# Q's and K's copies on ScalarE in the first self-attention, and an earlier context split, Q transfers on two queues and a second PSUM bank for V at the cross-attention's begin

## The reference

```python
x = x + L0_xattn(layernorm(x), ctx)       # x @ W1.T + mean(ctx) @ W2.T + b
x = x + L0_attn(layernorm(x), ...)        # 16 heads of 32, causal band of 128
x = x + L0_ffn(layernorm(x), ...)         # 16 experts, top 4, and a shared one
x = x + L1_xattn(layernorm(x), ctx, ctx)  # softmax over the 256 queries (axis=1)
x = x + L1_attn(layernorm(x), ...)        # windows of 128, shifted by 64
x = x + L1_ffn(layernorm(x), ...)         # 8 experts, top 2

# L0_attn
q, k, v = split(x @ Wqkv.T + bqkv)
probs = softmax(where(band, q @ k.T / sqrt(32), -inf))
y = (probs @ v) @ Wo.T + bo

# L1_xattn
Q = query @ Wq + bq;  K = ctx @ Wk + bk;  V = ctx @ Wv + bv
attn = softmax(einsum('bihd,bjhd->bijh', Q, K) * SCALE, axis=1)
out = einsum('bijh,bjhd->bihd', attn, V) @ Wo + bo
```

## Time and profile before

| | kernel before |
|---|---|
| runs (us) | 2662.23, 2661.63, 2662.91; median 2662.23 |
| profiled execution (us) | 2662.88 |
| its span, first to last instruction (us) | 2661.2 |
| mean granted TensorE clock (1 is full) | 0.992 |
| busy (us): PE, PEld | 2608.1, 2202.5 |
| busy (us): DVE, ACT, POOL | 1971.5, 1862.7, 1272.0 |
| chain of waits that ended last | PE 95%, DVE 2%, ACT 1%, DMA 1% |

### The profile page before, as it was taken

The page is one execution under the profiler, slowest core; times in us unless marked ns, Lnnn a source line. Parts: engine busy times, 40 slices in busy tenths (PEclk is TensorE's granted clock), DMA queues, the critical chain, the costliest instruction groups (busy, mean ns, idle before and its releaser), DMA issues.

```text
span 2661.2 us, 59615 instructions
## 1 busy us (share of the span) xinstructions
PE 2608.1 (98%) x21096; PEld 2202.5 (83%) x21096; DVE 1971.5 (74%) x3890; ACT 1862.7 (70%) x6826; POOL 1272.0 (48%) x2199
## 2 busy tenths in 40 slices
PE   8998999899999999999999999999999998999998
PEld 6875999788888888888888888888888885799997
DVE  8876866577787777787777787777787776655555
ACT  2213444288888888888888888888888886355553
POOL 4532111165655565655665655656655653222222
PEclk9998999999999999999999999999999999999999
DMA  9992554556666656666666666666666652545451
GB/s 385 388 396 97 196 190 167 135 154 182 157 161 173 164 157 160 165 162 167 161 166 158 158 169 168 160 158 168 154 164 168 167 130 109 187 177 190 184 190 72
DMA packets 132301, 473.34 MB, mean 178 GB/s; under 512 B 31128, under 2 KB 31256, under 8 KB 124832
## 3 DMA queue, kind: packets, MB, share of 16 engines
q1 hardware_dynamic: 122400, 451.69, 57.9%
q10 hardware_dynamic: 9600, 17.83, 1.8%
HBM read 244.47 MB, written 17.30 MB: 98 GB/s over the span
## 4 chain that ended last, share of the span: by engine, by line
PE 95%; DVE 2%; ACT 1%; DMA 1%; issue 0%; POOL 0%; ACTq 0%; SPq 0%; DVEq 0%; POOLq 0%
PE PB L587 21%; PE PB L612 15%; PE PB L620 14%; PE PB L600 14%; PE PB L688 7%; PE PB L703 6%; PE PB L416 6%; PE PB L549 6%; PE PB L562 3%; PE PB L445 1%; PE PB L476 1%; DMA AR<-in_ctx 1%; ACT EE L832 1%; PE PB L452 1%; PE PB L497 0%
## 5 line engine op out<-in xcount | busy, mean ns | idle before, releaser
L832 ACT ACTIVATE EE<-PB,small 128x256 f32<-128x256 f32 x3136 | 1445.1, 482 | 204.8 <-DVE small L1217 191.4
L1217 DVE TENSOR_REDUCE small<-PB 128x2 f32<-128x512 f32 x1568 | 1031.5, 682 | 355.3 <-PE PB L612 355.1
L832 ACT ACTIVATION_READ_ACCUMULATOR EE<-PB,small 128x1 f32 x3136 | 665.0, 212 | 0.0
L1478 POOL TENSOR_TENSOR VS<-V,small 128x128 f32<-128x128 f32 x784 | 320.5, 409 | 689.4 <-DVE small L1223 682.1
L587 PE MATMUL PB<-CTX,WKV 128*128 128x256 f32 x4704 | 624.7, 282 | 3.1 <-POOL CTX L1466 3.1
L587 PEld LDWEIGHTS PB<-CTX,WKV 128*128 128x128 f32 x4704 | 588.1, 190 | 3.4 <-POOL CTX L1466 3.3
L612 PEld LDWEIGHTS PB<-QS,STK 128*128 128x128 f32 x3136 | 469.1, 190 | 122.0 <-issue 79.9
L612 PE MATMUL PB<-QS,STK 128*128 128x256 f32 x3136 | 555.1, 288 | 5.3 <-ACT EE L832 5.2
L600 PE MATMUL PB<-WKV,CTX 128*128 128x512 f32 x1584 | 433.9, 396 | 3.0 <-DVE V L1213 3.0
L620 PE MATMUL PB<-EE,VS 128*32 128x256 f32 x6272 | 381.4, 384 | 0.0
L600 PEld LDWEIGHTS PB<-WKV,CTX 128*128 128x128 f32 x1584 | 274.0, 191 | 40.0 <-DVE V L1213 3.9
(11 more groups left out here) (201 smaller groups left out, 2546.3 us busy)
## 6 DMA issues: line engine op xcount, KB each, us to landing
STK<-KHL SPq DMA_DIRECT2D x1568, 128.0 KB, 2.5
RW<-in_l1f SPq DMA_DIRECT2D x32, 2048.0 KB, 8.1
AR<-in_ctx SPq DMA_DIRECT2D x49, 1024.0 KB, 8.5
RAW<-in_ctx SPq DMA_DIRECT2D x98, 512.0 KB, 3.7
WF<-in_l0f SPq DMA_DIRECT2D x17, 2304.0 KB, 8.9
v_scr<-RAW ACTq DMA_DIRECT2D x64, 256.0 KB, 7.6
V<-v_scr SPq DMA_DIRECT2D x64, 256.0 KB, 2.9
WA<-in_l0a SPq DMA_DIRECT2D x1, 4096.0 KB, 13.9
```

What stands on the lines that cost most here:

```text
L832: m = e.activation(EE[:, b, s, :], bank(2 * (k % 2) + half, 256 * (s % 2), 256), ACT.Exp, bias=nm[:, b, s:s + 1], accum_out=su[:, b, s:s + 1])
L1217: e.tensor_reduce(nm[:, k % RING, 2 * half:2 * half + 2], bank(2 * (k % 2) + half).rearrange("p (s i) -> p s i", s=2), axis=AX.X, op=ALU.m ...
L1478: e.tensor_tensor(VS[:, b, :].rearrange("p (s d) -> p s d", s=4), V[:, t % 4, 128 * c:128 * c + 128].rearrange("p (s d) -> p s d", s=4), r ...
```

## The change

It has two parts, in different stages.

*First self-attention.* The eight copies of Q and K move from VectorE to ScalarE for u = 0: five ahead of the first exponentials, two between those of chunk 0 and 1, one between those of chunk 1 and 2. ScalarE applies scale before bias, so the bias of Q is multiplied by SCALE once, on GpSimd (`bq`). VectorE's list is maxima, reciprocals and V's copies alone. TensorE projects the first half of V before the last scores. ScalarE's first FFN split moves behind all exponentials, GpSimd's behind the diagonals.

*Cross-attention's begin.* The high half of context group 2 is made right after Q is split, before the low halves of K (and GpSimd's low half, which waits for it, so can run then). Q's transfers: SP issues strips 0 to 2 (12 transfers), ScalarE strip 3 (4 transfers) between and behind its copies of K. The second V (n = 1) uses bank 7, so its matmuls wait for an old copy of bank 7 (`k_lo` 4) and no longer for the first V's copy. The bias of X is added at k = 8 and 9 of the loop.

```diff
+        bq = sb("bq", [P, NC])
+        VBANK = {1: 7}
-        def stack_q(e, half):
-            for s in range(2 * half, 2 * half + 2):
-                for q in range(4):
+        def stack_q(e, s, quarters):
+            for q in quarters:
 # sync_program
-            stack_q(e, 0)
+            for s in range(3):
+                stack_q(e, s, range(4))
 # tensor_program, attention(A)
                     if c + 1 < NC:
                         project(c + 1, 0)
+                    elif u == 0:
+                        values(0)
                     scores(c)
-                values(0)
+                if u:
+                    values(0)
                 values(1)
 # tensor_program, project_v(n, part)
-                    if n:
+                    if n == 1:
+                        w.wait_ge("k_lo", 4)
+                    elif n:
                         w.wait_ge("v_out", n)
-                    m = e.matmul(bank(5), CTX[:, g % 3, xh, c, j:j + 128], WKV[:, 2 + wh, c, :],
+                    m = e.matmul(bank(VBANK.get(n, 5)), CTX[:, g % 3, xh, c, j:j + 128], WKV[:, 2 + wh, c, :],
 # scalar_program, attention(A)
+                def project_out(c, qk):
+                    w.wait_ge("qk_mm", 8 * u + 2 * c + qk + 1)
+                    src = bank(6 + qk, 0, 256)
+                    if qk:
+                        m = e.activation(A.KT[:, c, :], src, ACT.Identity, bias=BC[:, A.ck + c:A.ck + c + 1])
+                    else:
+                        m = e.activation(A.QT[:, c, :], src, ACT.Identity, bias=bq[:, c:c + 1], scale=SCALE)
+                    m.then_inc(S["qk_out"], 1)
+
+                after = ((2, 1), (3, 0)), ((3, 1),), (), ()
+                if u == 0:
+                    w.wait_ge("d_bc", 16)
+                    w.wait_ge("bq_scaled", 1)
+                    for c, qk in ((0, 0), (0, 1), (1, 0), (1, 1), (2, 0)):
+                        project_out(c, qk)
...
+                    if u == 0:
+                        for p in after[c]:
+                            project_out(*p)
 # scalar_program
             move_xt(1)
+            attention(attn[0])
             split0(0, 0)
-            attention(attn[0])
             split0(0, 1)
...
-                if ch == 1:
+                if ch:
                     w.wait_ge("q_split", 1)
-                    stack_q(e, 1)
+                    stack_q(e, 3, ((0,), (1,), (2, 3))[ch - 1])
 # vector_program, attention(A): the old list stands under "else"
+                if u == 0:
+                    maxima(0)
+                    maxima(1)
+                    reciprocals(0)
+                    maxima(2)
+                    reciprocals(1)
+                    values_out(0)
+                    maxima(3)
 # vector_program, before and in the loop
+            split_hi(2)
             for ch, kb in enumerate(KBANK[1]):
                 k_lo(1, ch, kb)
             for n in range(2):
                 v_out(n)
-            w.wait_ge("d_bi0", 32)
-            for i in range(2):
-                e.tensor_tensor(X[:, i, :], X[:, i, :], BI[:, BSLOT[R_XO], :], ALU.add).then_inc(S["x_xbias"], 1)
-            split_hi(2)
...
+                if k in (8, 9):
+                    w.wait_ge("d_bi0", 32)
+                    e.tensor_tensor(X[:, k - 8, :], X[:, k - 8, :], BI[:, BSLOT[R_XO], :], ALU.add).then_inc(S["x_xbias"], 1)
 # gpsimd_program
+            w.wait_ge("d_bc", 16)
+            e.tensor_scalar(bq[:, :], BC[:, C_L0Q:C_L0Q + NC], SCALE, None, ALU.mult).then_inc(S["bq_scaled"], 1)
...
-            w.wait_ge("ln_xn", 4)
+            attention(attn[0])
             split0(0)
-            attention(attn[0])
             split0(1)
```

More of the change, by code:

```diff
@@ L43 @@
 wkv_hi wv_dve wv_pool wk_pool sums early_hi early_lo early_mm early_out p1_mm x_bias mean_rhs mean_mm x_mean
-qk_mm qk_out av_mm av_out x_abias sc_mm sc_max sc_exp sc_rcp diag turn_mm turn_out amix_mm amix_out ao_mm x_attn
+bq_scaled qk_mm qk_out av_mm av_out x_abias sc_mm sc_max sc_exp sc_rcp diag turn_mm turn_out amix_mm amix_out ao_mm x_attn
 f0_xs f0_xs_act f0_hi f0_lo f0_plo f0_up f0_silu f0_mul f0_hhi f0_hlo f0_dn f0_acc gate_mm gate_sig gate_comb
@@ L245, in build @@
         lg1, rk1, t81 = (small[:, o:o + 16] for o in (112, 128, 144))
-        def stack_q(e, half):
-            for s in range(2 * half, 2 * half + 2):
-                for q in range(4):
-                    e.dma_start(
-                        QS[32 * q:32 * q + 32, s, :, :].bitcast(F32),
-                        QHL[32 * s:32 * s + 32, q // 2, :, :].bitcast(F32)).then_inc(S["d_q"], 16)
+        def stack_q(e, s, quarters):
+            for q in quarters:
+                e.dma_start(
+                    QS[32 * q:32 * q + 32, s, :, :].bitcast(F32),
+                    QHL[32 * s:32 * s + 32, q // 2, :, :].bitcast(F32)).then_inc(S["d_q"], 16)
         def sync_program(e):
@@ L1011, in attention @@
                 w.wait_ge(f"d_bi{BSLOT[A.rv]}", 16 * (u + 1))
-                project_out(0, 0)
-                project_out(0, 1)
-                project_out(1, 0)
-                maxima(0)
-                project_out(1, 1)
-                project_out(2, 0)
-                maxima(1)
-                project_out(2, 1)
-                project_out(3, 0)
-                reciprocals(0)
-                maxima(2)
-                project_out(3, 1)
-                maxima(3)
-                reciprocals(1)
-                values_out(0)
+                if u == 0:
[6 more added lines that the diff above has]
+                    maxima(3)
+                else:
+                    project_out(0, 0)
+                    project_out(0, 1)
+                    project_out(1, 0)
+                    maxima(0)
+                    project_out(1, 1)
+                    project_out(2, 0)
+                    maxima(1)
+                    project_out(2, 1)
+                    project_out(3, 0)
+                    reciprocals(0)
+                    maxima(2)
+                    project_out(3, 1)
+                    maxima(3)
+                    reciprocals(1)
+                    values_out(0)
                 reciprocals(2)
@@ L1212, in v_out @@
                     w.wait_ge("vs", 4 * (t - 4) + 4)
-                e.tensor_tensor(V[:, t % 4, :], bank(5), BI[:, BSLOT[R_XV], :], ALU.add).then_inc(S["v_out"], 1)
+                e.tensor_tensor(V[:, t % 4, :], bank(VBANK.get(n, 5)), BI[:, BSLOT[R_XV], :], ALU.add).then_inc(S["v_out"], 1)
             def maxima(k, half):
```

## The result

| | median us | lowest to highest | runs |
|---|---|---|---|
| before | 2661.63 | 2661.04 to 2662.91 | 9 |
| changed | 2655.65 | 2650.19 to 2656.52 | 9 |

The ratio is 0.9974, with the interval 0.9965 to 0.9983: 6.0 us faster by the medians, 6.9 by the ratio. That is as forecast in sign and within the range (2650.5 to 2656.8), 2.05 us above the forecast. New is the scatter: 6.3 us between runs, where before had 1.9.

A forecast was written before the change was run, and what follows sets the result against it. TensorE was taken as the bound (95% of the chain of waits), with nothing to gain in the long loop. 3.2 us (first self-attention) plus 5.4 (cross-attention's begin) made 8.6 off 2662.23: 2653.6 us, range 2650.5 to 2656.8.

The forecast's parts named there:

- Part A: First self-attention: ScalarE copies Q and K, half of V projected before the last scores; 3.2 us gained, bounds 2.0 and 3.6.
- The 0.4 us wait of the third scores: First self-attention: TensorE ready at 222.2, ScalarE's copy of K chunk 2 done at 222.6, so 0.4 us of waiting stays.
- The 0.2 us for VectorE's lateness: End of first self-attention: VectorE's last maxima, reciprocal and V copy make the turned blocks 0.2 us late, leaving 3.2 of 3.4.
- The waits of 2.22 and 3.08: Cross-attention's begin: TensorE's waits for V's bank (2.22 us) and context group 2's low half (3.08 us) would both go.
- part B: Cross-attention's begin: reordered copies, split and Q transfers start mixing at 523.7 instead of 529.18; 5.4 us gained.
- Q's landing: Cross-attention's begin: TensorE waits for all 16 Q transfers, set by bandwidth; first scores at 515.9, bounds 513.4 and 518.
- rival 1: Cross-attention's begin: issue sets Q's end, Q lands early at 514.1, no clock lost; gain 11.5 us, 2650.7; chance 0.12.
- the clock: Cross-attention's begin: after 2.5 us idle TensorE runs at 1.2 GHz once; 1.0 us lost, bounds 0 and 1.7.
- The bracket before the first scores: Cross-attention: sign to look for, a TensorE wait of 2 to 2.5 us with a DMA as its releaser.
- 2 (Q at 518): Cross-attention's begin: SP's last pieces land late, first scores at 518, full slow stretch behind; gain 5.9 us, 2656.3; chance 0.15.
- 3: First self-attention: K's copy waits behind exponentials instead of maxima, half the gain (1.6); with Q late too, 2657.9; chance 0.08.
- 4: Long loop: ScalarE starts without its lead and paces it; at 0.02 us per k 7.1 us slower, 2669.3; chance 0.03.

The follow-up runs named there:

- kernel 10: Changed kernel with ScalarE's copies kept, but the first V product in self-attention moved back behind the last scores; 2658.12 us, ratio 0.9985.
- kernel 6: Changed kernel with V's second tile back in bank 5, waiting for the copy of the first; 2651.46 us, ratio 0.996.
- kernel 7: Changed kernel with Q's 16 transfers divided as before, 8 on SP and 8 on ScalarE; 2655.00 us, ratio 0.9973.
- kernel 9: Changed kernel with the context's third split back behind VectorE's two V copies; 2653.35 us, ratio 0.9966.
- kernel 1: Changed kernel with the cross-attention changes taken back, leaving only the first self-attention changes; 2658.28 us, ratio 0.9983.
- kernel 4: Changed kernel with each of Q's 16 transfers halved to 64 KB, the attention using half of Q twice; 2650.19 us, ratio 0.9954.
- kernel 12: Changed kernel with a 512 KB context load moved behind Q's 12 transfers on SP, plus dummy products at three places outside cross-attention; 2646.48 us, ratio 0.9943.
- kernel 8: Changed kernel with dummy products on TensorE in six of its idle stretches; 2661.94 us, ratio 0.9999.
- kernel 3: Changed kernel with 18 dummy products on TensorE in front of the cross-attention's wait for Q; 2651.30 us, ratio 0.9958.

## Why the prediction was right, and what was off

- **Part A, 3.2 forecast, 3.34 measured.** First scores to turned blocks 19.6 forecast, 19.66 measured. That it fits so well is partly luck. The 0.4 us wait of the third scores didn't come, because TensorE was not ready earlier: two projections take 3.65 us from start to start (218.63 to 222.28 in the changed kernel), not 2 x 1.73. The 1.73 came from durations, whose modelled ends reach 0.07 us past the next start for two projections and 0.16 for one. The missing wait and the longer work cancel. The 0.2 us for VectorE's lateness didn't show either: 3.34 is gained at the turned blocks and at the output alike. The moved V product hid K's last copy, as said; kernel 10's profile shows what is left without it.
- **The waits of 2.22 and 3.08 went, 0.78 stayed**: right. But kernels 6, 7 and 9 show that each of part B's three pieces can be undone for 0 to 1 us; with all undone (kernel 1) the begin takes 23.3 us again. They are several ways to the same point, Q's landing. Pairs of them were not tried.
- **Q's landing, the next bound.** Forecast 515.9 in the times of before; 506.06 + (511.93 - 502.33) = 515.66. "So bandwidth, not the issue" is borne out against rival 1: last pieces that are issued 5.4 (before) and 8.6 us (changed kernel) after SP's first both land 12.6 to 12.8 us after it, and kernel 4 halves the bytes. (The Trainium skill, "DMA: Bandwidth & Descriptors", section "Where 436 GB/s comes from", has 435 GB/s as the ceiling of such transfers; the windows of the changed kernel above show 197 to 219.) What the working left out stands ahead of its window: SP issued a 512 KB load at 502.34, which landed 4.2 us later, at 506.5, just ahead of Q's first pieces. Moving it brought Q an estimated 1.6 us nearer (kernel 12 against 8).
- **The mis-sized term: the clock.** Forecast "at 1.2 GHz once, partly over the idle time: 1.0 us lost (bounds 0 and 1.7)". The profiled run lost 9.42 - 6.82 = 2.60 us, beyond the upper bound: the slow time was 6.84 us, twice the stretch of 3.4 that before showed and that the bound was taken from, and nearly all of it lay over work. So B gave 4.1 instead of 5.4. Kernel 3 takes the wait's idle time away, nothing else, and gets the 2.6 us back. The trace of before had longer slow stretches at other places, which could have set the bound (window of before, columns as above):

```profile
262.50:268.50 6.00, 4.52 (x20) 4.16 (x21) 4.29 (x5) 2.91 (x4) 0.06 (x1) 0.50 0.64 221
```

- **X's bias.** Forecast "0, at worst 1.3"; it costs 0.5 us, in its own block of the loop (rows above).
- **Signs that came otherwise.** The bracket before the first scores is 1.99 us (2 to 2.5 forecast) and says "issue", not a DMA; only in kernel 3 does the profile name the DMA. First V product to first mixing is 19.0 us, not 17.7, and 5.8 us of work run slow, not 2.
- **The scatter** was not foreseen. With one or two slow stretches at this place scores to mixing take 1.5 to 2.8 us longer than with none. Other places add to it: mean clocks of 0.992 and 0.996 differ by an estimated 21 us of slow time, three times what this place has. The lowest run, 2650.19 at a clock of 0.996, is near rival 1's 2650.7, but probably by another way: no clock lost, Q not early. It was not profiled.
- **Rivals.** 2 (Q at 518) did not come. 3 is answered by kernel 1. 4 is out: the loop's window has 353.78 us of ScalarE in both, and the first mixing to the end took 0.6 us more, not 8.

## What to carry over

A wait on the path costs itself and then what TensorE's clock does behind it: price it with whole slow stretches of both sizes that the trace shows, not with the mildest one. Where several pieces lead to one later bound, find that bound's own cause first (here Q's bytes and those ahead of it in a queue); the pieces before it are worth little one by one. A wait can be filled with work as well as shortened: with real work (the product that kernel 10 takes back) or with dummies, as long as they delay nothing (kernels 3 and 12 against 8).

## What the runs showed of the hardware

- Round a last wait of 1.99 to 2.64 us the granted clock fell to 0.50 for 3.4 or 6.8 us, after 0.21 to 1.00 it stayed at 1.00 (table above); behind kernel 10's wait of 1.63 it fell for 3.4. Why it is once 3.4 and once 6.8 stays open.
- Q's 2 MB from SBUF to SBUF were there 11.7 to 13.7 us after SP's first issue, whether ScalarE issued four or eight of the pieces, and 10.8 us after it without the 512 KB load ahead; the spread among kernels with the same transfers is not explained.
- A product of 256 columns with f32 tiles took two rows in the trace, with fp32r tiles one: 8.37 us for 19 (kernel 8), 2.31 us for 18 (kernel 3).
